# One-rounding quantisation in the mx layer, and causal attention stepped one sequence at a time

## The chip, the cores and the metric

One program on one core of a Trainium2 chip, in one launch. The metric is the device time of that core in microseconds. Its engines are named as in the profile: PE (TensorE; PEld is its weight load), DVE (VectorE), ACT (ScalarE), POOL (GpSimd) and SP (SyncE, which issues DMAs). Every engine runs its own instructions in order; they meet at semaphores.

## What is computed

Sixteen sequences of 256 tokens with 128 features pass through twelve stages (`load`, `gla`, `swiglu`, `mx_linear`, `causal_attention`, `router1`, `experts1`, `rope_attention`, `ternary_mlp`, `mamba`, `router3`, `experts3`). Every layer works on normalised rows and adds its result to `x`. Two stages matter here.

`mx_linear` quantises its input rows and its weight in blocks of 32 to the nearest value of a 6-bit grid (exact ties go down) and multiplies:

```python
def _mx_quantize(t, eps=1e-30):
    rows, K = t.shape
    blocks = t.reshape(rows, K // BLOCK_SIZE, BLOCK_SIZE)
    scales = jnp.maximum(jnp.max(jnp.abs(blocks), axis=-1) / FP6_E2M3_MAX, eps)
    q = _nearest_on_grid(blocks / scales[..., None], _GRID)
    return (q, scales)
```

`causal_attention` is, for each sequence, a single head of width 128: q, k and v are products of the normalised rows with `Wq`, `Wk`, `Wv` plus biases, the scores of a token with itself and earlier tokens go through a softmax, the weighted sum of v goes through `Wo`, plus a bias. Since the weights of a row sum to 1, the bias of v adds the same vector, bias times `Wo`, to every row of the result.

## The kernel before

`x` stays in SBUF, [128 partitions, 32 tiles of 128]; a sequence is two tiles. `g.mv` holds mean and variance of every row. Between two stages `Signals.close` (L56 to L62) lets POOL clear each semaphore of the stage, and all engines wait for that.

Both stages begin with `Norm`: DVE adds epsilon to the 32 variance columns, POOL raises them all to the power -0.5 (L205, `g.rs`), and DVE waits for it. `normalised` (L958) then makes the normalised rows of a sequence with two DVE instructions (L961). Both stages take two sequences, u = 0 and 1, per turn of a loop, eight turns in all, and work through each operation for u = 0, then for u = 1. Both end a turn with `Finish.vector` (L234 to L241), the statistics of the new rows of `x`, on DVE.

`mx_linear`: a turn on DVE is `quantised(i + 1)`, then `added(i)`. `quantised` is a `Chain` of 15 steps, each waiting for the step before of its own sequence: normalise, and in `mx_quantise` block maxima, scale, reciprocal, multiply; two clamps and two subtractions that cut a value in three parts; and for all three parts (768 elements per partition) a rounding (L998), its error (L1002), a test for ties (L1006) and a correction (L1010); then two additions and the scale. PE transposes the result (L1095), ACT copies it (L1083), PE multiplies with `wT` (L1103) and adds the bias by a product with a row of ones (L1104, a contraction over one row), and DVE adds it to `x` (L1063).

`causal_attention`: each sequence has four PSUM banks of its own, reused within a turn. Order of a turn: PE projects q, k (L1245, L1246) and v with its bias by a row of ones (L1252, L1253), ACT copies q and k out (L1213, L1214), PE makes scores (L1257, L1258), DVE masks them (L1159), takes maxima (L1163, L1164) and negates them (L1167), ACT takes exponentials (L1218, L1220), PE transposes (L1263), ACT copies (L1224), PE makes the context (L1270 to L1272), DVE copies it (L1175), PE multiplies with `Wo` (L1277), DVE divides and adds the bias (L1181), adds to `x` (L1187) and does the statistics. The normalised and transposed tokens of the next turn are made in the middle of this one. PE's v products of the next turn wait for this turn's result.

## Time and profile before

| what | value |
|---|---|
| median of 3 runs | 3184.25 us (3179.88 to 3189.71) |
| the profiled execution | 3185.84 us, span 3184.0 us |
| PE, DVE, ACT, POOL busy | 71%, 62%, 40%, 36% of the span |
| granted clock of PE, mean over the span | 0.841 |
| `mx_linear`, first to last instruction | 951.86 to 1098.24 us |
| `causal_attention`, first to last instruction | 1100.50 to 1235.27 us |

The stages follow one another with a stop of all engines between them, so the busy shares of the whole span say little of the two stages that the change touches; they are read from views of their own windows. A row `A:B` of a windows view gives a stretch's length, each engine's busy time in it with its number of instructions, the mean granted clock of PE (1.00 is 2.4 GHz, 0.50 is 1.2 GHz), the DMA engines' share and GB/s.

### The profile page before, as it was taken

What the parts mean: (1) busy time and instruction counts of PE and PEld (TensorE: products, weight loads), DVE (VectorE), ACT (ScalarE), POOL (GpSimd) and SP (SyncE); (2) the same over time, 40 slices, a digit from 0 to 9 for tenths busy, and PEclk for the clock granted to TensorE, in tenths of its full rate; (3) what the DMA queues carried; (4) which work ended last, traced back from release to release, by engine and by line L of the source; (5) the groups of instructions that cost most, each with busy time, mean ns of one, the idle gap of its engine ahead of it and who ended that gap; (6) DMA issues with size and microseconds to landing.
All of it is one profiled execution on the core that took longest, in us unless ns stands there. A gap on an engine that the chain in (4) does not pass through costs nothing. (4 is left out here: it accounts for less than half of the span.)

```text
span 3184.0 us, 47196 instructions
## 1 busy us (share of the span) xinstructions
PE 2253.1 (71%) x15094; PEld 1544.5 (49%) x15094; DVE 1972.1 (62%) x5353; ACT 1271.6 (40%) x2663; POOL 1153.3 (36%) x1205
## 2 busy tenths in 40 slices
PE   2899999999883485149189885748888889651290
PEld 0566666666672364037155553635555555440170
DVE  3677777777669754201466663858888888744016
ACT  2455454554330042013044553337777777410130
POOL 2342342433210001545211111137777777513551
PEclk9899999999995587579578887869999999855595
DMA  7300000000010000112323231000000000000122
GB/s 212 94 1 0 0 0 0 0 0 0 14 47 0 0 0 0 34 56 64 90 70 78 66 96 39 0 1 1 0 0 0 0 0 0 1 0 22 50 62 79
DMA packets 105855, 93.75 MB, mean 29 GB/s; under 512 B 12268, under 2 KB 92294, under 8 KB 105606
## 3 DMA queue, kind: packets, MB, share of 16 engines
q1 hardware_dynamic: 98086, 76.85, 8.8%
q0 software_dynamic: 7680, 15.81, 1.5%
q8 instruction: 45, 0.74, 0.1%
q14 instruction: 44, 0.36, 0.0%
HBM read 62.15 MB, written 46.26 MB: 34 GB/s over the span
## 5 line engine op out<-in xcount | busy, mean ns | idle before, releaser
L2713 POOL TENSOR_SCALAR mb_w<-mb_duT,mb_bT 128x256 f32<-128x256 f32 x512 | 463.8, 924 | 144.9 <-PE bank L2723 133.6
L2649 DVE TENSOR_TENSOR_SCAN mb_hs<-mb_dA,bank 128x512 f32<-128x512 f32 x256 | 300.6, 1203 | 31.5 <-issue 24.6
L38 POOL TENSOR_TENSOR scrap<-ones 128x1 f32<-128x1 f32 x96 | 19.8, 207 | 814.0 <-DVE gla_ss L420 487.4
L2742 PE MATMUL bank<-mb_hc,ident 128*128 128x512 f32 x512 | 251.6, 614 | 24.7 <-DVE mb_hc L2659 23.5
L1993 DVE TENSOR_REDUCE ra_mx<-bank 128x2 f32<-128x512 f32 x256 | 166.7, 687 | 99.5 <-PE bank L1870 98.1
L2704 ACT ACTIVATE mb_dA<-mb_delta,mb_A 128x255 f32<-128x255 f32 x512 | 217.6, 494 | 3.6 <-DVE mb_hs L2649 3.4
L2079 ACT ACTIVATE ra_pT<-bank 128x512 f32<-128x512 f32 x256 | 139.4, 596 | 129.4 <-PE bank L1890 128.5
L1644 ACT ACTIVATE e_hid<-bank,e_b 128x512 f32<-128x512 f32 (+1 forms) x128 | 81.1, 634 | 234.5 <-PE bank L1663 231.5
L2723 PE MATMUL bank<-ident,mb_w 128*128 128x128 f32 x1024 | 149.4, 280 | 35.6 <-DVE mb_hs L2649 26.2
L1627 POOL DMA_INDIRECT results<-e_y,e_x x112 | 107.2, 957 | 144.6 <-DVE e_y L1698 119.6
L1655 PE MATMUL bank<-ident,e_x 128*128 128x128 f32 x112 | 18.8, 292 | 197.3 <-DMA e_x<-queue 197.3
L2659 DVE TENSOR_TENSOR mb_hc<-mb_hs,bank 128x1024 f32<-128x1024 f32 x128 | 152.8, 1194 | 0.0
L2723 PEld LDWEIGHTS bank<-ident,mb_w 128*128 128x128 f32 x1024 | 117.0, 145 | 58.5 <-issue 45.3
L546 DVE COPY_PREDICATED gla_sT<-c_seen,bank 128x384 f32<-128x384 int32 x256 | 134.4, 576 | 12.1 <-issue 12.1
L2742 PEld LDWEIGHTS bank<-mb_hc,ident 128*128 128x128 f32 x512 | 88.1, 192 | 106.8 <-issue 62.2
L1692 DVE COPY e_xT<-bank 128x512 f32<-128x512 f32 (+1 forms) x32 | 19.7, 616 | 185.9 <-PE bank L1655 185.8
L532 DVE TENSOR_TENSOR gla_qm<-bank,gla_ex 128x256 f32<-128x256 f32 x128 | 53.9, 421 | 123.3 <-ACT gla_en L514 123.3
L1698 DVE TENSOR_TENSOR e_y<-bank,e_b 128x512 f32<-128x512 f32 (+1 forms) x32 | 20.0, 625 | 166.4 <-PE bank L1673 166.4
L1870 PE MATMUL bank<-ra_k,ra_q 48*128 48x256 bf16 x512 | 97.5, 304 | 33.4 <-DMA ra_q<-rope_rows 26.2
L1889 PE MATMUL bank<-ra_q,ra_k 48*128 48x256 bf16 x512 | 111.3, 298 | 9.5 <-ACT ra_neg L2072 8.3
L420 DVE TENSOR_REDUCE gla_ss<-gla_sq 128x8 f32<-128x512 f32 x128 | 87.0, 679 | 42.4 <-ACT gla_sq L398 40.5
L387 ACT ACTIVATE gla_az<-gla_az 128x512 f32<-128x512 f32 x64 | 40.3, 630 | 179.0 <-DVE gla_az L415 179.0
(516 smaller groups left out, 6234.8 us busy)
## 6 DMA issues: line engine op xcount, KB each, us to landing
results<-const_empty SPq DMA_DIRECT2D x2, 4096.0 KB
e_got<-results SPq DMA_DIRECT2D x32, 256.0 KB, 3.3
rope_rows<-ra_part SPq DMA_DIRECT2D x48, 128.0 KB, 2.0
ra_k<-rope_rows SPq DMA_DIRECT2D x32, 192.0 KB, 3.3
ra_q<-rope_rows SPq DMA_DIRECT2D x32, 192.0 KB, 4.3
queue<-const_spare_rows SPq DMA_DIRECT2D x1, 4128.0 KB
...
```

Of the source, the lines that this page charges most:

```text
L546: dve.copy_predicated(sT[b][:, hd, :], g.seen[:, :], SC[hd][:, 0:3 * P]).then_inc(sc_ready, 1)
L1627: pool.indirect_dma_start(out=results[:, :], in_=y[u % YR][:, t, :], in_offset=None, out_offset=bass.IndirectOffsetOnAxis(ap=x[e % XR][:, ...
L1870: ins = pe.matmul(MX[a][:, t * 256:(t + 1) * 256], qz[k][rows, p, t * P:(t + 1) * P], kk[k][rows, p, :], start=True, stop=True)
L1889: pe.matmul(out, kk[k][rows, p, t * P:(t + 1) * P], qz[k][rows, p, :], start=True, stop=False)
L1993: dve.tensor_reduce(mx[:, :, a, p], halves(MX[a]), AXX, ALU.max).then_inc(mx_ready, 1)
L2079: act.activation(pT[p % 4][a][:, :, :], halves(SB[a]), ACT.Exp, scale=SC).then_inc(p_ready, 1)
L2649: dve.tensor_tensor_scan(hs[n // 2 % 2][:, n % 2, :, :].rearrange("p c t -> p (c t)"), dA[n % RD][:, :, :].rearrange("p c t -> p (c t)"), ...
L2659: dve.tensor_tensor(hc[grp % 2][:, :, :, :], hs[grp % 2][:, :, :, :], RC[grp % 2][:, :].rearrange("p (n t) -> p n t", n=2).unsqueeze(2) .b ...
L2704: ins = act.activation(dA[n % RD][:, c, 1:SEQ], delta[k][:, c, 1:SEQ], ACT.Exp, scale=A[:, c, n:n + 1])
L2713: ins = pool.tensor_scalar(w[n % RH][:, h, :], duT[k][:, h, :], bT[k][:, h, n:n + 1], None, ALU.mult)
L2723: ins = pe.transpose(DB[n % 2][:, c * 256 + h * P:c * 256 + (h + 1) * P], w[n % RH][:, h, c * P:(c + 1) * P], g.ident[:, :])
L2742: ins = pe.matmul(YB[:, :], g.ident[:, :], hc[grp % 2][:, j, :, :].rearrange("p c t -> p (c t)"), start=(n == 0), stop=(n == NS - 1))
```

## The change

In `mx_quantise`, the three parts are gone. The power of two of each value (its exponent bits, by a bitwise and; at least 8) is kept in `p`, its inverse is made by a bitwise exclusive or, the value is multiplied with it, rounded once by adding a large constant in two ways of which the lower result is kept, multiplied back with `p` and scaled. This makes 13 steps, without normalising. Normalising moves to ACT as one activation per tile (`normalised_rows`), the addition of `x` moves to PE as a product with the identity, and ACT copies the sum back to `x`. The power -0.5 is taken in two parts, 4 tiles and then 28.

In `causal_attention` each purpose has one PSUM bank (`XT, QK, VB, SB, PT, CB, OB`), used by all sequences in turn; SBUF tiles stay doubled. A step works on one sequence s: PE projects s+1, makes the result of s-1, transposes the weights of s and the tokens of s+2, makes the scores of s+1 and the context of s. Semaphores are counted per sequence. Normalising and the copy of the context move from DVE to ACT. The bias of v is multiplied with `Wo` once, ahead of the steps, and added to the output bias (`bo`). The rolled loops make 5 turns of two steps; 2 steps ahead of them and 4 behind them are written out.

```diff
--- before.py
+++ after.py
...
-def mx_quantise(chain, x, y, amax, sc, z, r, t, n):
...
+def mx_quantise(chain, x, out, amax, sc, back, y, p, w, v, n):
...
-    return lambda: (chain.step(lambda u: dve.tensor_tensor(y[u][:, 0:w], y[u][:, 0:w], r[u][:, 2, 0:w], ALU.add)),
-                    chain.step(lambda u: dve.tensor_tensor(blocks(x[u]), blocks(y[u][:, 0:w]), wide(sc[u][:, :]),
-                                                           ALU.mult)))
+    chain.step(lambda u: dve.tensor_scalar(back[u][:, 0:n], sc[u][:, 0:n], 0.5, None, ALU.mult))
+    chain.step(lambda u: dve.reciprocal(amax[u][:, 0:n], sc[u][:, 0:n]))
+    chain.step(lambda u: dve.tensor_tensor(blocks(cols(y[u])), blocks(x[u]), wide(amax[u][:, 0:n]), ALU.mult))
+
+    chain.step(lambda u: dve.tensor_scalar(cols(p[u]).bitcast(I32), cols(y[u]).bitcast(I32), MX_EXP, None,
+                                           ALU.bitwise_and))
+    chain.step(lambda u: dve.tensor_scalar(cols(p[u]), cols(p[u]), 8.0, None, ALU.max))
+    chain.step(lambda u: dve.tensor_scalar(cols(w[u]).bitcast(I32), cols(p[u]).bitcast(I32), MX_EXP, None,
+                                           ALU.bitwise_xor))
+    chain.step(lambda u: dve.tensor_tensor(cols(w[u]), cols(y[u]), cols(w[u]), ALU.mult))
+
+    chain.step(lambda u: dve.tensor_scalar(cols(v[u]), cols(w[u]), MX_ODD, -0.25, ALU.add, ALU.add))
+    chain.step(lambda u: dve.scalar_tensor_tensor(out=cols(v[u]), in0=cols(w[u]), scalar=MX_EVEN, in1=cols(v[u]),
+                                                  op0=ALU.add, op1=ALU.min))
+    chain.step(lambda u: dve.scalar_tensor_tensor(out=cols(v[u]), in0=cols(v[u]), scalar=-MX_EVEN, in1=cols(p[u]),
+                                                  op0=ALU.add, op1=ALU.mult))
+    chain.step(lambda u: dve.tensor_tensor(blocks(out[u]), blocks(cols(v[u])), wide(back[u][:, 0:n]), ALU.mult))
...
 def mx_linear(nc, g):
...
         def _(dve):
...
-            mx_quantise(ch, w, [y[0]], [amax[0][:, 0:4]], [sc[0][:, 0:4]], z, r, t, 4)()
+            moments = g.mv[:, :].rearrange("p (t k) -> p t k", k=2)
+            dve.tensor_scalar(var[:, :], moments[:, :, 1], LN_EPS, None, ALU.add).then_inc(var_ready, 1)
+            dve.wait_ge(rs_ready, 1)
+            dve.scalar_tensor_tensor(out=nmr[:, early], in0=moments[:, early, 0], scalar=-1.0, in1=g.rs[:, early],
+                                     op0=ALU.mult, op1=ALU.mult).then_inc(nmr_ready, 1)
+            ch = Chain(dve, [wq_steps], 0, MX_STEPS, items=(0,))
+            mx_quantise(ch, [g.mx_w[:, :]], [wd[:, :]], amax, sc, back, y, p, w, v, 4)
             ch.close()
...
+            dve.wait_ge(rs_ready, 2)
+            dve.scalar_tensor_tensor(out=nmr[:, later], in0=moments[:, later, 0], scalar=-1.0, in1=g.rs[:, later],
+                                     op0=ALU.mult, op1=ALU.mult).then_inc(nmr_ready, 1)
...
             def quantised(i):
-                if not isinstance(i, int):
-                    for u in U:
+                for u in U:
+                    if not isinstance(i, int):
                         dve.wait_ge(xT_psum[u], i)
-                ch = Chain(dve, steps, i, MX_STEPS + 3)
-                ch.step(lambda u: normalised(dve, g, xn[u], i * 2 + u, g.rs))
-                mx_quantise(ch, flat, y, amax, sc, z, r, t, 8)()
+                    dve.wait_ge(xn_ready[u], i + 1)
+                ch = Chain(dve, steps, i, MX_STEPS)
+                mx_quantise(ch, x_in, x_out, amax, sc, back, y, p, w, v, 8)
                 ch.close()
+
+            def finished(i):
+                for u in U:
+                    fin.vector(dve, u, i, i * 2 + u, x_ready[u])
+
+            quantised(0)
+            with dve.Fori(0, NSEQ // 2 - 1) as i:
+                quantised(i + 1)
+                finished(i)
+            finished(NSEQ // 2 - 1)
+
+        @block.gpsimd
+        def _(pool):
+            pool.wait_ge(var_ready, 1)
+            for part in (early, later):
+                pool.tensor_tensor(g.rs[:, part], var[:, part], g.neg_half[:, part], ALU.pow).then_inc(rs_ready, 1)
+
...
+            def normalised_rows(i):
+                for u in U:
+                    s = i * 2 + u
+                    if not isinstance(i, int) or i:
+                        act.wait_ge(steps[u], (i - 1) * MX_STEPS + MX_READ)
+                    for h in range(2):
+                        ins = act.activation(xn[u][:, h, :], g.x[:, ds(s * (2 * P) + h * P, P)], ACT.Identity,
+                                             bias=scale_of(nmr, s * 2 + h), scale=scale_of(g.rs, s * 2 + h))
+                    ins.then_inc(xn_ready[u], 1)
+
+            def transposed(i):
+                for u in U:
+                    act.wait_ge(xT_psum[u], i + 1)
+                    act.activation(xT[u][:, :], T[u][:, 0:256], ACT.Copy).then_inc(xT_ready[u], 1)
...
+                    act.wait_ge(o_psum[u], i + 1)
+                    act.activation(g.x[:, seq_cols(s)], O[u][:, 0:256], ACT.Copy).then_inc(x_ready[u], 1)
+
+            act.wait_ge(nmr_ready, 1)
+            normalised_rows(0)
+            act.wait_ge(wT_psum, 1)
+            act.activation(wT[:, :], T[0][:, 0:P], ACT.Copy).then_inc(wT_ready, 1)
+            act.wait_ge(nmr_ready, 2)
+            normalised_rows(1)
+            transposed(0)
+            added(0)
+            with act.Fori(1, NSEQ // 2 - 1) as i:
+                normalised_rows(i + 1)
+                transposed(i)
                 added(i)
+            transposed(NSEQ // 2 - 1)
             added(NSEQ // 2 - 1)
...
             def product(i):
                 for u in U:
-                    pe.wait_ge(steps[u], i * (MX_STEPS + 3) + MX_STEPS + 3)
+                    pe.wait_ge(steps[u], i * MX_STEPS + MX_STEPS)
                     for h in range(2):
-                        ins = pe.transpose(T[u][:, h * P:(h + 1) * P], xn[u][:, h, :], g.ident[:, :])
+                        ins = pe.transpose(T[u][:, h * P:(h + 1) * P], xd[u][:, h, :], g.ident[:, :])
                     ins.then_inc(xT_psum[u], 1)
                 for u in U:
+                    s = i * 2 + u
                     if not isinstance(i, int) or i:
                         pe.wait_ge(x_ready[u], i)
                     pe.wait_ge(xT_ready[u], i + 1)
                     for h in range(2):
                         o = O[u][:, h * P:(h + 1) * P]
                         pe.matmul(o, xT[u][:, h * P:(h + 1) * P], wT[:, :], start=True, stop=False)
+                        pe.matmul(o, g.ident[:, :], g.x[:, ds(s * (2 * P) + h * P, P)], start=False, stop=False)
                         ins = pe.matmul(o, g.ones[0:1, :], g.mx_b[:, :], start=False, stop=True)
                     ins.then_inc(o_psum[u], 1)
...
+
+    def over(s, n):
+        return not isinstance(s, int) or s >= n
+
+    def pe_tokens(pe, s, u):
+        pe.wait_ge(xn_ready, s + 1)
+        if over(s, 1):
+            pe.wait_ge(xT_ready, s)
+        for h in range(2):
+            ins = pe.transpose(XT[:, h * P:(h + 1) * P], xn[u][:, h, :], g.ident[:, :])
+        ins.then_inc(xT_psum, 1)
+
+    def pe_project(pe, s, u):
+        pe.wait_ge(xT_ready, s + 1)
+        if over(s, 1):
+            pe.wait_ge(qk_ready, s)
+        pe.matmul(QK[:, 0:256], g.l1_Wq[:, :], xT[u][:, :], start=True, stop=True)
+        pe.matmul(QK[:, 256:512], g.l1_Wk[:, :], xT[u][:, :], start=True, stop=True).then_inc(qk_psum, 1)
+        if over(s, 1):
+            pe.wait_ge(v_ready, s)
+        for h in range(2):
+            ins = pe.matmul(VB[:, h * P:(h + 1) * P], xT[u][:, h * P:(h + 1) * P], g.l1_Wv[:, :], start=True,
+                            stop=True)
+        ins.then_inc(v_psum, 1)
+
+    def pe_scores(pe, s, u):
+        pe.wait_ge(qk_ready, s + 1)
+        if over(s, 1):
+            pe.wait_ge(sm_ready, s)
+        pe.matmul(SB[:, 0:P], q[u][:, 0:P], k[u][:, 0:P], start=True, stop=True)
+        pe.matmul(SB[:, P:3 * P], q[u][:, P:2 * P], k[u][:, :], start=True, stop=True).then_inc(s_psum, 1)
+
...
+            pe.wait_ge(cT_ready, s)
+        pe.matmul(CB[:, 0:P], v[u][:, 0:P], pT[u][:, 0:P], start=True, stop=True)
+        pe.matmul(CB[:, P:2 * P], v[u][:, 0:P], pT[u][:, P:2 * P], start=True, stop=False)
+        pe.matmul(CB[:, P:2 * P], v[u][:, P:2 * P], pT[u][:, 2 * P:3 * P], start=False, stop=True).then_inc(c_psum, 1)
+
+    def pe_result(pe, s, u):
+        pe.wait_ge(cT_ready, s + 1)
+        if over(s, 1):
+            pe.wait_ge(z_ready, s)
+        for h in range(2):
+            ins = pe.matmul(OB[:, h * P:(h + 1) * P], cT[u][:, h * P:(h + 1) * P], g.l1_Wo[:, :], start=True, stop=True)
+        ins.then_inc(o_psum, 1)
+
...
+    def act_exp(act, s, u):
+        act.wait_ge(nmx_ready, s + 1)
+        if over(s, 2):
+            act.wait_ge(rinv_ready, s - 1)
+        act.activation(sm[u][:, 0:P], sm[u][:, 0:P], ACT.Exp, bias=mx[u][:, 0:1], accum_out=sums[u][:, 0:1])
+        act.activation(sm[u][:, P:3 * P], sm[u][:, P:3 * P], ACT.Exp, bias=mx[u][:, 1:2],
+                       accum_out=sums[u][:, 1:2]).then_inc(p_ready, 1)
...
+    def dve_maxima(dve, s, u):
+        dve.wait_ge(sm_ready, s + 1)
+        if over(s, 2):
+            dve.wait_ge(p_ready, s - 1)
+        dve.tensor_reduce(mx[u][:, 0:1], sm[u][:, 0:P], AXX, ALU.max)
+        dve.tensor_reduce(mx[u][:, 1:2], sm[u][:, P:3 * P], AXX, ALU.max).then_inc(mx_ready, 1)
+
+    def dve_offsets(dve, s, u):
+        dve.wait_ge(mx_ready, s + 1)
+        dve.tensor_scalar(mx[u][:, :], mx[u][:, :], -1.0, None, ALU.mult).then_inc(nmx_ready, 1)
...
+    def dve_divided(dve, s, u):
+        dve.wait_ge(rinv_ready, s + 1)
+        dve.wait_ge(o_psum, s + 1)
+        for h in range(2):
+            ins = dve.scalar_tensor_tensor(out=z[u][:, h * P:(h + 1) * P], in0=OB[:, h * P:(h + 1) * P],
+                                           scalar=rinv[u][:, h:h + 1], in1=bo[:, :], op0=ALU.mult, op1=ALU.add)
+        ins.then_inc(z_ready, 1)
+
...
+    def pe_step(pe, s, u, back=True, on=True, far=True):
+        w = 1 - u
+        if on:
+            pe_project(pe, s + 1, w)
+        if back:
+            pe_result(pe, s - 1, w)
+        pe_weights(pe, s, u)
+        if far:
+            pe_tokens(pe, s + 2, u)
+        if on:
+            pe_scores(pe, s + 1, w)
+        pe_context(pe, s, u)
+
+    def act_step(act, s, u, back=True, on=True, far=True, farther=True):
+        w = 1 - u
+        if back:
+            act_context(act, s - 1, w)
+        act_exp(act, s, u)
+        if on:
+            act_qk(act, s + 1, w)
+        act_weights(act, s, u)
+        if far:
+            act_tokens(act, s + 2, u)
+        if farther:
+            act_normalised(act, s + 3, w)
+
+    def dve_step(dve, s, u, back=True, on=True):
+        w = 1 - u
+        if on:
+            dve_values(dve, s + 1, w)
+        dve_inverse(dve, s, u)
+        if back:
+            dve_divided(dve, s - 1, w)
+            dve_result(dve, s - 1, w)
+            dve_stats(dve, s - 1, w)
+        if on:
+            dve_masked(dve, s + 1, w)
+        if back:
+            dve_moments(dve, s - 1, w)
+        if on:
+            dve_maxima(dve, s + 1, w)
+        if back:
+            dve_keep(dve, s - 1, w)
+        if on:
+            dve_offsets(dve, s + 1, w)
+
+    def steps(eng, step, ends):
+        step(eng, 0, 0, back=False)
+        step(eng, 1, 1)
+        with eng.Fori(1, NSEQ // 2 - 2) as i:
+            for u in U:
+                step(eng, i * 2 + u, u)
+        for s in range(NSEQ - 4, NSEQ):
+            step(eng, s, s % 2, **{name: s + n <= last for name, n in ends.items()})
 
     with nc.Block() as block:
...
+                dve.scalar_tensor_tensor(out=nmr[:, tiles], in0=moments[:, tiles, 0], scalar=-1.0, in1=g.rs[:, tiles],
+                                         op0=ALU.mult, op1=ALU.mult).then_inc(nmr_ready, 1)
+                if part == 0:
+                    dve.wait_ge(bv_psum, 1)
+                    dve.tensor_copy(bv[:, :], OB[:, 0:1]).then_inc(bv_ready, 1)
+                    dve_values(dve, 0, 0)
+                    dve_masked(dve, 0, 0)
+                    dve_maxima(dve, 0, 0)
+                    dve_offsets(dve, 0, 0)
+                    dve.wait_ge(bo_psum, 1)
+                    dve.tensor_tensor(bo[:, :], OB[:, P:2 * P], g.l1_bo[:, :], ALU.add).then_inc(bo_ready, 1)
+            dve.wait_ge(bo_ready, 1)
+            steps(dve, dve_step, {"on": 1})
+            dve_divided(dve, last, 1)
+            dve_result(dve, last, 1)
+            dve_stats(dve, last, 1)
+            dve_moments(dve, last, 1)
+            dve_keep(dve, last, 1)
 
         @block.gpsimd
...
-                attended(i)
-            attended(NSEQ // 2 - 1, False)
+            pe.matmul(OB[:, 0:1], g.l1_bv[:, :], g.ones[0:1, 0:1], start=True, stop=True).then_inc(bv_psum, 1)
+            pe_tokens(pe, 0, 0)
+            pe_project(pe, 0, 0)
+            pe_tokens(pe, 1, 1)
+            pe_scores(pe, 0, 0)
+            pe.wait_ge(bv_ready, 1)
+            pe.matmul(OB[:, P:2 * P], bv[:, 0:1].broadcast_to([P, P]), g.l1_Wo[:, :], start=True, stop=True)\
+                .then_inc(bo_psum, 1)
+            pe.wait_ge(bo_ready, 1)
+            steps(pe, pe_step, {"on": 1, "far": 2})
+            pe_result(pe, last, 1)
     sb.close()
     sig.close()
```

## Rows read from the trace of the kernel before

**Rows 1.** Windows: start of mx_linear, the rest of it, causal_attention.

```profile
951.86:963.65 11.79, 0.47 (x1) 0.18 (x1) 5.24 (x21) 0.00 (x0) 5.43 (x1) 0.50 0.00 0
963.65:1098.24 134.59, 55.76 (x160) 37.40 (x160) 122.56 (x465) 6.13 (x16) 0.00 (x0) 0.50 0.00 0
1100.50:1235.27 134.77, 100.70 (x496) 79.77 (x496) 72.99 (x306) 49.51 (x135) 5.42 (x1) 0.83 0.00 0
```

**Rows 2.** Timeline of mx_linear on DVE: start, length, instruction, [idle before].

```profile
990.82 0.74 DVE L1063 TENSOR_TENSOR x<-bank,x 128x256 f32 x2
...
1007.22 0.74 DVE L1063 TENSOR_TENSOR x<-bank,x 128x256 f32 x2
...
1010.69 1.18 DVE L961 TENSOR_SCALAR mx_xn<-x,mv,rs 128x128 f32 x4 [0.72 <-issue]
...
1011.78 0.74 DVE L982 TENSOR_REDUCE mx_amax<-mx_xn 128x8 f32<-128x256 f32 x2
...
1012.88 0.76 DVE L986 TENSOR_TENSOR mx_y<-mx_xn,mx_amax 128x256 f32<-128x256 f32 x2
1013.56 0.28 DVE L989 TENSOR_SCALAR mx_z<-mx_y 128x256 f32<-128x256 f32 x1
...
1015.71 1.29 DVE L998 TENSOR_SCALAR mx_r<-mx_z 128x256 f32<-128x256 f32 x6
```

**Rows 3.** Groups by line and form: the nearest other shapes for new instructions.

```profile
L2510 DVE SCALAR_TENSOR_TENSOR mb_delta<-mb_z,mb_az 128x512 f32<-128x512 f32 x16 | 11.1, 692 | 22.1 <-ACT mb_az L2588 22.1
...
L1635 POOL TENSOR_TENSOR e_rs<-e_ve,neg_half 128x4 f32<-128x4 f32 x8 | 8.1, 1011 | 58.1 <-DVE e_ve L1740 58.1
```

**Rows 4.** Timeline of PE at half clock, last products of mx_linear.

```profile
1090.14 0.79 PE L1103 MATMUL bank<-mx_wT,mx_xT 128*128 128x128 f32 x2
...
1090.86 0.79 PE L1104 MATMUL bank<-mx_b,ones 1*128 1x128 f32 x2
```

**Rows 5.** Timeline of PE at half clock, last turn of causal_attention.

```profile
1229.34 0.55 PEld L1270 LDWEIGHTS bank<-ca_pT,ca_v 128*128 128x128 f32 x2
...
1229.76 0.55 PEld L1271 LDWEIGHTS bank<-ca_pT,ca_v 128*128 128x128 f32 x2
```

**Rows 6.** Timeline of ACT in an earlier stage: a table load and its activation.

```profile
117.22 1.28 ACT L513 ACT_TABLE_LOAD   x1
118.52 0.39 ACT L513 ACTIVATE gla_ex<-bank 128x264 f32<-128x264 f32 x1
```

**Rows 7.** Waits at the starts of causal_attention and of the router.

```profile
DVE ca_norm_t L189 <- PEq L57: 2.3, 1, 2.3
...
DVE r_norm_t L189 <- PEq L57: 4.4, 1, 4.4
```

**Rows 8.** Timeline of causal_attention at full clock: one turn's length, and its legs.

```profile
1172.85 0.42 DVE L1175 COPY ca_cT<-bank 128x256 f32<-128x256 f32 x1 [1.55 <-PE bank L1272]
...
1175.62 0.47 ACT L1213 ACTIVATE ca_q<-bank,ca_bqs 128x256 f32<-128x256 f32 x1 [1.54 <-PE bank L1246]
...
1179.69 0.49 PE L1257 MATMUL bank<-ca_k,ca_q 128*128 128x128 f32 x2
...
1180.65 1.21 DVE L1159 TENSOR_TENSOR ca_sm<-bank,c_causal 128x384 f32<-128x384 f32 x2 [0.43 <-PE bank L1258]
...
1183.01 0.40 ACT L1218 ACTIVATE ca_sm<-ca_sm,ca_mx 128x128 f32<-128x128 f32 x1 [3.84 <-DVE ca_mx L1167]
...
1184.05 0.31 PEld L1263 LDWEIGHTS bank<-ident,ca_sm 128*128 128x128 f32 x3 [3.19 <-ACT ca_sm L1220]
...
1186.62 0.42 DVE L1175 COPY ca_cT<-bank 128x256 f32<-128x256 f32 x1 [1.55 <-PE bank L1272]
```

**Rows 9.** Windows within causal_attention: PE's granted clock against its busy time.

```profile
1136.00:1140.00 4.00, 1.22 (x6) 0.57 (x5) 3.37 (x14) 1.87 (x9) 0.00 (x0) 0.80 0.00 0
...
1180.00:1195.00 15.00, 11.89 (x70) 9.16 (x68) 9.87 (x40) 6.24 (x17) 0.00 (x0) 1.00 0.00 0
1112.00:1120.00 8.00, 8.00 (x23) 5.88 (x22) 1.41 (x3) 0.84 (x2) 0.00 (x0) 0.50 0.00 0
```

327 lines of the change are left out of this document (131 added, 196 removed).

## The prediction

> **What bounds the kernel now.** The page says only that PE is busy 71% of the span. Both changed stages stand alone between two stops of all engines, so I read their windows first [rows 1]. In `mx_linear` DVE is busy 122.56 of 134.59 us and PE has 0.50 of its clock throughout: DVE bounds it, and only shorter DVE work helps. `causal_attention` takes 134.77 us with PE busy 100.70 and DVE 72.99: no engine is full. The timeline shows why: two sequences pass through the same legs one behind the other, one turn taking 1186.62 - 1172.85 = 13.77 us at full clock, 6.9 per sequence, with DVE idle 1.55 us ahead of the context copy while PE works, PE idle 3.19 us ahead of the weights' transposes while DVE and ACT work, and ACT idle 3.84 us ahead of the exponential [rows 8]. It is a chain of latencies, with PE as the longest user.
>
> **mx_linear: the chain.** A turn takes 1007.22 - 990.82 = 16.40 us. From 1007.22 to 1010.69 come two additions, the statistics and a loop gap of 0.72, 3.47 us together; the other 12.93 are the 15 steps [rows 2]. Prices for both sequences of a step, start to start: a two-source instruction of 256 elements 1013.56 - 1012.88 = 0.68; a one-source one 0.40 (six in 1.29, the last 0.28, so 0.20 each); block maxima, scale and reciprocal 1012.88 - 1011.78 = 1.10, of which a tiny step is (1.10 - 0.68) / 2 = 0.21 [rows 2]. The new chain has maxima and three tiny steps, 1.31; five two-source steps, 3.40; four one-source steps, 1.62 with rounding: 6.33 us. Two prices are not shown. No wide integer instruction with one source is in the trace; below it is the f32 one-source 0.40, above it the two-source 0.68. I take 0.40, the nearest in operands and size; the upper end adds 2 x 0.28 x 8 = 4.5 us. The scalar-tensor-tensor takes 0.692 us for 512 elements [rows 3], which agrees with 0.42 for 256; I price it as two-source. The page "Vector Engine (DVE) Microarchitecture Reference" of the Trainium skill, section 5.1, lets any one-source instruction between SBUF tiles take the two-port mode; by that rule the integer steps cost 0.40.
>
> So eight chains save 8 x 6.60 = 52.8 us, and the additions, 0.67 a turn, leave DVE in six turns: 4.0. Normalising in ACT is at no cost to DVE, since ACT was busy 6.13 us in the whole stage [rows 1]; it is queued behind `added`, which I come to below.
>
> **mx_linear: both ends.** Before, the first chain starts 11.79 us into the stage: a power of 5.43 us, then the weight's chain [rows 1]. A power over 4 columns takes 1.01 us [rows 3]; the weight's 13 steps (about 3.7 us alone, one-item steps) now lie beside the power of the other 28 columns, which ends near 5.8, and the first chain starts near 6.3: 5.5 saved. At the end PE and ACT are exposed. PE at half clock passes from a 128-row product to a one-row product in 1090.86 - 1090.14 = 0.72 us [rows 4], and between two 128-row products in 0.42 [rows 5]. A tile now has `xT`, identity, ones: 0.42 + 0.72 + 0.72 = 1.86, four tiles 7.5, transposes and copy 1.2, the last copy 0.4, the statistics 0.95: 10.1 us after the last chain, where it was 9.1. Loss 1.0.
>
> Sum for `mx_linear`: 52.8 + 4.0 + 5.5 - 1.0 = 61.3 us. The turn becomes 6.33 + 2.80 = 9.13 us, and PE needs 8.7 of it, ACT some 4 plus a table load. ACT ends `added` 9.1 after a chain, loads a table if the loop head asks for one (1.28), normalises in 1.5, and is done 11.9 after that chain; DVE wants the rows at 9.13 + 2.80 = 11.9. It just fits, so it is late next.
>
> **causal_attention: the step.** A step is a cycle: exponential of s, copy of q and k of s+1, scores of s+1, mask, maxima, negation, then exponential of s+1. Legs [rows 8]: ACT is through with an exponential after 0.89 (its data reach PE after 1184.05 - 1183.01 = 1.04); q and k 0.37 + 0.47 = 0.84 and 0.06 to PE; scores 1180.65 - 1179.69 = 0.96. From mask to exponential two sequences take 1183.01 - 1180.65 = 2.36; for one, with the old sequence's aggregates between, it lies between 1.18 and 2.36, and instruction by instruction (mask 0.6, aggregates 0.25, maxima 0.6, negation 0.2) I take 1.65. Sum 4.40 us against 6.9. Beside it must fit: on DVE the v copy, inverse, division, addition and two statistics, which are through some 2.8 us after the exponential's start, just when the scores come; on ACT weights, tokens, normalising (0.74) and the context copy, through just ahead of the next exponential; on PE 3.7 us at full clock (q, k 0.86, v 0.44, scores 0.65, transposes 0.6, context 0.66, result 0.5). The v products lose their one-row partner, which by the same switch made a v of 0.42 per product out of 0.22: 1.2 us of PE per sequence gone.
>
> A loop head asks for one table load in each of 5 turns of two steps; ACT then comes to the exponential 0.6 late, 3.0 us in all, with a load of 1.28 and its activation 118.52 - 117.22 = 1.30 after its start [rows 6]. The page "ScalarE: Activation LUTs" of the Trainium skill, "What ACT_TABLE_LOAD costs", adds a drain of 1.38 us to each load; the row shows 0.02. By the page five turns here would cost 6.9 us more.
>
> At half clock PE needs 7.2 a step and bounds it. Before, the clock was 0.50 over 1112 to 1120 with PE busy all 8 us, and fell again in a stretch with 1.22 of 4 us busy; over 1180 to 1195, 11.89 of 15 busy, it stayed 1.00 [rows 9]. The new step has no such idle stretch and no one-row products, so I expect a later clock mostly at 1.00, with one to three steps at half clock at first.
>
> **causal_attention: the sum.** Ahead of the steps 10.0 us (power of 4 columns 1.3, normalise, transpose, project, scores, mask, two bias products at half clock); the first step 7.2; fourteen of 4.40, 61.6; table loads 3.0; from the last exponential to the last statistic 7.0: 88.8, and 97.2 with three more steps at half clock. I take 95, a saving of 39.8. Fewer semaphores, 30 for 50: DVE waited 2.3 us at the stop that clears 24 and 4.4 at the one that clears 50 [rows 7], 0.08 each, so 1.7 less.
>
> Total 61.3 + 39.8 + 1.7 = 102.8. The profiled execution took 3185.84, its span 3184.0; 3185.84 - 102.8 = 3083.0, and as it lies 1.6 over the median, I forecast 3082 us.
>
> **Rivals.**
> - *PE or ACT bounds the mx turn* (0.08). If identity products also cost 0.72, four tiles cost 1.2 us more, the turn grows to some 10.3: 3082 + 8 x 1.15 = 3091. For it: 8.7 of 9.13 is thin. Against: rows 5 show 0.42 for just such neighbours.
> - *Half clock throughout causal_attention* (0.10). 16 x 7.2 + 17 = 132: 3119. For it: 8 busy us at 0.50; against: the rise later in that stage [rows 9].
> - *Cross waits in the step* (0.07). DVE reaches the mask late, as inverse and division stand in its queue ahead of it and wait for ACT and PE; a step of 6.0 adds 24: 3106.
> - *Each table load stops ACT longer* (0.03). A stop the size of a load, 5 loads here and 6 halved in `mx_linear`, is 8 x 1.3 = 10: 3092. The row speaks against it. The drain of the skill's page would be this rival.
> - *Slower* (0.02). One bank per purpose makes each step wait for all legs of its sequence, so nothing overlaps. The old turn is such a pass, 13.77 for two; at 13 per step the stage takes 16 x 13 + 3 = 211, 76 more than before: 3185.8 - 61.3 - 1.7 + 76 = 3199. It decides from (134.8 + 63 - 17) / 16 = 11.3 us a step. Against it: the code has PE project s+1 before it needs the weights of s.
> - *No change* (0.01) would need a step near 11.
> The likeliest case has the rest, 0.69, with its own range 3066 to 3100.
>
> **Range and chances.** Below, `mx_linear` with PE at full clock (-3), attention at 89 with no table cost (-9) and smaller gaps give 3066, with a margin for the estimated fill 3062. Above, slow integers (+4.5), three half-clock steps (+2) and cross waits (+24) reach 3113, and 3116 leaves out little but the clock rival. Three in a thousand (0.3%, about what a measurement of this kernel can tell from no change) is 9.6 us, far inside the forecast: faster 0.97, same 0.01, slower 0.02.
>
> **What would show it.** In the new profile: an mx chain of 6.3 us and a turn of 9.1 us; the integer steps at 0.28 us an instruction; `mx_linear` some 85 us long; exponentials 4.4 to 5.0 us apart, the stage some 95 us long at a clock near 0.9; the router's wait about 2.7 us. Wrong would be: DVE waiting for normalised rows in `mx_linear`, integer steps at 0.41, exponentials 6 us or more apart, or 0.50 of clock far into the attention.

## The result, and the profile after

The changed kernel takes 3082.48 us, the median of four runs (3071.34 to 3087.23), against 3185.32 before: a ratio of 0.9673 [0.9642, 0.9704]. The forecast was 3082. Two of its terms were off, though, by 7 and by 13 us in opposite directions, and most of what follows is about them.

The profiled execution is the one of 3071.34 us, the fastest of the four, with a span of 3069.2. Windows of the changed kernel: `mx_linear`, `causal_attention`, all that follows, and three stretches of the attention. They answer to [rows 1] and [rows 9].

```profile
951.17:1043.39 92.22, 69.38 (x225) 51.48 (x225) 68.81 (x336) 24.35 (x65) 5.77 (x2) 0.50 0.00 0
1045.51:1127.16 81.65, 69.50 (x436) 59.02 (x436) 55.78 (x262) 58.43 (x177) 5.77 (x2) 0.94 0.00 1
...
1130.14:3069.20 1939.06, 1275.64 (x7685) 861.66 (x7685) 1110.24 (x2513) 794.40 (x1646) 840.06 (x981) 0.80 0.12 33
...
1045.50:1049.50 4.00, 1.61 (x5) 1.13 (x6) 0.50 (x4) 1.68 (x5) 3.73 (x2) 0.50 0.01 4
1049.50:1053.50 4.00, 3.85 (x16) 3.05 (x15) 0.76 (x2) 1.57 (x4) 2.04 (x1) 0.70 0.00 0
1053.50:1121.50 68.00, 61.64 (x406) 53.15 (x406) 50.89 (x238) 54.31 (x167) 0.00 (x0) 1.00 0.00 0
```

`mx_linear` went from 146.38 to 92.22 us and is no longer full on DVE, which is busy 68.81 us of it; PE, at 0.50, is now as busy as DVE. `causal_attention` went from 134.77 to 81.65 us, and PE's clock is 1.00 from 8 us into the stage up to 1121.5, a step before its end. The wait that answers to [rows 7] shrank by 1.4:

```profile
DVE r_norm_t L189 <- PEq L57: 3.0, 1, 3.0
```

The timeline of `mx_linear` after, one turn on three engines; it answers to [rows 2].

```profile
957.36 0.75 DVE L989 TENSOR_REDUCE mx_amax<-mx_xn 128x8 f32<-128x256 f32 x2
...
1005.11 0.74 DVE L989 TENSOR_REDUCE mx_amax<-mx_xn 128x8 f32<-128x256 f32 x2 [0.69 <-ACT mx_xn L1084]
1005.30 0.80 PE L1133 MATMUL bank<-mx_wT,mx_xT 128*128 128x128 f32 x2 [1.62 <-ACT mx_xT L1091]
...
1007.11 0.49 DVE L996 TENSOR_SCALAR mx_p<-mx_y 128x256 int32<-128x256 int32 x2
...
1011.42 0.28 DVE L234 BATCH_NORM_STATS2 mx_fin_st<-x 128x6 f32 x1
...
1012.79 1.11 PE L1124 MATMUL bank<-ident,mx_xd 128*128 128x128 f32 x4
1013.01 0.38 ACT L1097 ACTIVATE x<-bank 128x256 f32 x1 [3.36 <-PE bank L1135]
1013.56 1.65 ACT L1084 ACTIVATE mx_xn<-x,mx_nmr,rs 128x128 f32 x4 [0.17 <-issue]
1015.11 0.63 ACT L1091 ACTIVATE mx_xT<-bank 128x256 f32<-128x256 f32 x2
1015.33 0.74 DVE L989 TENSOR_REDUCE mx_amax<-mx_xn 128x8 f32<-128x256 f32 x2 [0.69 <-ACT mx_xn L1084]
1015.52 0.79 PE L1133 MATMUL bank<-mx_wT,mx_xT 128*128 128x128 f32 x2 [1.61 <-ACT mx_xT L1091]
```

The chain is 1011.42 - 1005.11 = 6.31 us, but the turn is 1015.33 - 1005.11 = 10.22. What ends each wait closes a loop through two engines, ACT and PE. ACT has stood 3.36 us before `added`, which waits for PE's products; behind it in its queue are the normalising of the next rows and the copy of `xT`. After `added` ACT first normalises four tiles (1013.56 to 1015.11), for which DVE then waits 0.69, and only then copies `xT`, for which PE has been idle 1.61 us. From the last copy of `added` in one turn to the same in the next it takes 0.38 + 0.17, then 1.55 of normalising, 0.41 to the first product, and 7.7 of products at half clock: 10.2.

The timeline of `causal_attention` after; it answers to [rows 8].

```profile
1055.79 1.28 ACT L1247 ACT_TABLE_LOAD   x1
1057.08 0.40 ACT L1247 ACTIVATE ca_sm<-ca_sm,ca_mx 128x128 f32<-128x128 f32 x1
...
1078.13 0.40 ACT L1247 ACTIVATE ca_sm<-ca_sm,ca_mx 128x128 f32<-128x128 f32 x1 [0.41 <-DVE ca_mx L1284]
...
1079.02 0.45 ACT L1240 ACTIVATE ca_q<-bank,ca_bqs 128x256 f32<-128x256 f32 x1
...
1079.89 0.49 PE L1194 MATMUL bank<-ca_k,ca_q 128*128 128x128 f32 x2
...
1080.85 0.56 DVE L1273 TENSOR_TENSOR ca_sm<-bank,c_causal 128x384 f32<-128x384 f32 x1
...
1082.39 0.40 ACT L1247 ACTIVATE ca_sm<-ca_sm,ca_mx 128x128 f32<-128x128 f32 x1 [0.41 <-DVE ca_mx L1284]
...
1120.17 0.40 ACT L1247 ACTIVATE ca_sm<-ca_sm,ca_mx 128x128 f32<-128x128 f32 x1 [0.41 <-DVE ca_mx L1284]
```

One step is 1082.39 - 1078.13 = 4.26 us, and the fifteen from the first exponential to the last are (1120.17 - 1057.08) / 15 = 4.21 each: exponential to q copy 0.89, q and k to scores 0.87, scores to mask 0.96, mask to exponential 1.54. The table load at 1055.79 is the only one of the stage; its activation starts 0.01 us after its end.

### The profile page after: what moved, and what is told of

Its sections match the earlier page's. It is cut to its first block and busy times, and to the rows that moved or that the text cites. A ratio compares the mean times of both kernels' runs of the same rounds, so it can differ in the third digit from the quotient of the medians.

```text
span 3069.2 us, 47277 instructions
## 1 busy us (share of the span) xinstructions
PE 2227.3 (73%) x15098; PEld 1531.8 (50%) x15098; DVE 1896.1 (62%) x5160; ACT 1299.1 (42%) x2754; POOL 1156.5 (38%) x1207
## 5 line engine op out<-in xcount | busy, mean ns | idle before, releaser
L2140 DVE TENSOR_REDUCE ra_mx<-bank 128x2 f32<-128x512 f32 x256 | 166.3, 686 | 95.9 <-PE bank L2017 94.3
L546 DVE COPY_PREDICATED gla_sT<-c_seen,bank 128x384 f32<-128x384 int32 x256 | 134.3, 576 | 12.1 <-issue 12.1
L2889 PEld LDWEIGHTS bank<-mb_hc,ident 128*128 128x128 f32 x512 | 88.2, 192 | 106.7 <-issue 62.4
L1802 PEld LDWEIGHTS bank<-ident,e_x 128*128 128x128 f32 x112 | 14.4, 152 | 201.7 <-DMA e_x<-queue 200.8
```

The costliest lines, as they stand in the source:

```text
L546: dve.copy_predicated(sT[b][:, hd, :], g.seen[:, :], SC[hd][:, 0:3 * P]).then_inc(sc_ready, 1)
L2140: dve.tensor_reduce(mx[:, :, a, p], halves(MX[a]), AXX, ALU.max).then_inc(mx_ready, 1)
L2889: ins = pe.matmul(YB[:, :], g.ident[:, :], hc[grp % 2][:, j, :, :].rearrange("p c t -> p (c t)"), start=(n == 0), stop=(n == NS - 1))
```

## The experiments

Stage lengths in this table are from the start of `mx_linear` to that of `causal_attention`, from there to the router's, and from there to the end of the span, each in the one profiled execution. The runs e1 to e4, e5 to e8 and e9 to e12 each shared a chip and their runs of the kernel before (3188.61, 3184.31 and 3188.19 us). A stage length is of one execution, a median of several, so the two need not differ by the same amount.

| kernel | median us | ratio [95%] | mx | attention | rest |
|---|---|---|---|---|---|
| before | 3185.3 | | 148.6 | 139.2 | 1944.3 |
| after | 3082.5 | 0.9673 [0.9642, 0.9704] | 94.3 | 84.6 | 1939.1 |
| e1 | 3125.3 | 0.9809 [0.9781, 0.9837] | 94.3 | 133.5 | 1943.9 |
| e2 | 3140.4 | 0.9855 [0.9825, 0.9885] | 148.7 | 86.7 | 1953.7 |
| e3 | 3133.7 | 0.9837 [0.9813, 0.9861] | 102.6 | 128.3 | 1947.3 |
| e4 | 3176.6 | 0.9968 [0.9956, 0.9980] | 148.6 | 127.1 | 1947.4 |
| e5 | 3082.3 | 0.9677 [0.9662, 0.9693] | 94.3 | 86.8 | 1948.5 |
| e6 | 3077.0 | 0.9662 [0.9648, 0.9675] | 89.3 | 84.9 | 1952.0 |
| e7 | 3074.1 | 0.9651 [0.9636, 0.9665] | 83.0 | 86.1 | 1951.7 |
| e8 | 3073.8 | 0.9652 [0.9637, 0.9666] | 85.0 | 84.1 | 1947.2 |
| e9 | 3100.4 | 0.9734 [0.9714, 0.9754] | 94.3 | 103.1 | 1947.5 |
| e10 | 3094.8 | 0.9702 [0.9682, 0.9723] | 94.3 | 100.1 | 1950.3 |
| e11 | 3186.5 (one execution) | | 148.7 | 136.2 | 1945.8 |
| e12 | 3092.6 | 0.9702 [0.9685, 0.9719] | 97.4 | 91.0 | 1952.7 |

### Which half of the change gives what

**e1** is the changed kernel with the attention of before, **e2** the kernel before with the attention of after.

```diff
 e1: after.py
-def causal_attention(nc, g):   # seven banks, one sequence a step
+def causal_attention(nc, g):   # of before.py
 e2: before.py
-def causal_attention(nc, g):
+def causal_attention(nc, g):   # of after.py
```

> Only mx_linear and its quantiser are the new ones, causal_attention is the old one. The change's own trace has mx_linear at 92.2 us (951.17 to 1043.39) where it was 146.4. If the stages are separate, this run is 54 us faster than before, about 3131 us, and its attention stays near 134.8 us. Rival: the busier PE of the new mx_linear hands the attention a warmer clock; then the old attention is over 5 us shorter here too, and part of what I put down to the attention's new order belongs to mx_linear.

> Only causal_attention is the new one, mx_linear is the old one. Separate stages: 53 us from the attention and 1.5 us from fewer semaphores to clear, about 3131 us, with the attention near 82 us and exponentials 4.2 us apart from the first on. Rival (clock handed over by the new mx_linear): the attention begins at half clock for some steps of 7 us and takes 90 us or more.

e1 was 63.3 us under the kernel before, where 54 were expected, and e2 48.2, where 54.5 were. `mx_linear` has its 94.3 us in e1 as in after, and the new attention its 86.7 in e2 as in e5, so each half carries its own gain. (In e2 one step took 5.74 us; the half clock for steps of 7 us and the 90 us of e2's rival did not come.) The two gains add up to 111.5 us, 9 more than the whole change brings. Of these, the profiles show 5.7: the old attention took 133.5 us in e1 and 139.2 before, with the same instructions. No stage shows the remaining 3. Its windows in e1, the whole stage and its first 20 us:

```profile
1046.50:1180.00 133.50, 95.09 (x496) 74.57 (x496) 73.06 (x306) 49.40 (x135) 5.43 (x1) 0.87 0.00 0
1046.50:1066.50 20.00, 13.33 (x36) 9.29 (x36) 2.88 (x10) 3.73 (x7) 5.43 (x1) 0.50 0.00 1
```

and in **e3**, which has only the new quantiser in the old frame of `mx_linear`:

```diff
 before.py, mx_linear
-                ch = Chain(dve, steps, i, MX_STEPS + 3)
+                ch = Chain(dve, steps, i, MX_STEPS + 1)
                 ch.step(lambda u: normalised(dve, g, xn[u], i * 2 + u, g.rs))
-                mx_quantise(ch, flat, y, amax, sc, z, r, t, 8)()
+                mx_quantise(ch, flat, flat, amax, sc, back, y, p, w, v, 8)
```

> The old kernel with the new quantiser alone; normalising, the addition to x and the old order stay on DVE. My prices: chain 6.33 + 1.09 for normalising = 7.4 us, turn 7.4 + 3.5 = 10.9 us, the stage 44 to 46 us shorter than 146.4, so about 3140 us. The change's own turn is 10.22 us, so all that moves to ACT and PE would be worth only some 0.7 us a turn. Rival: additions wait for PE (7.1 us of products against a chain of 7.4) and the turn is 12 us or more; then the moves are worth much more.

```profile
1055.10:1183.40 128.30, 89.28 (x496) 70.77 (x496) 73.02 (x306) 48.98 (x135) 5.42 (x1) 0.91 0.00 0
1055.10:1075.10 20.00, 10.45 (x48) 7.68 (x49) 5.97 (x22) 6.37 (x18) 5.42 (x1) 0.75 0.00 1
```

The old stage is the shorter the more of it PE has its full clock: a mean of 0.82, 0.87 and 0.91 goes with 139.2, 133.5 and 128.3 us. So the gain of the new attention is 42 to 55 us, by how the old one was caught. The 5.7 us in e1 are what its rival asked for (over 5 us, from the busier PE of the new `mx_linear`), but that cause doesn't fit: in e3 PE was busy only 56 of the 100 us of `mx_linear`, against 69 of 91 in e1, and the old attention was shorter still. What makes the clock rise earlier in one execution than in another isn't shown; `mx_linear` ran at 0.50 ahead of all three. This is also why e3 is 55 us faster and not the 45 expected: its stage of `mx_linear` gained what was forecast. e3 also divides the gain of `mx_linear`: the shorter chain alone brings 46.0 of its 54.3 us, with a turn of 10.85 us, and the move of normalising, addition and power 8.3 more.

**e4** takes only the bias of v out of the old attention's steps.

```diff
 before.py, causal_attention
-                        pe.matmul(o, xT[u][:, h * P:(h + 1) * P], g.l1_Wv[:, :], start=True, stop=False)
-                        ins = pe.matmul(o, g.ones[0:1, :], g.l1_bv[:, :], start=False, stop=True)
+                        ins = pe.matmul(o, xT[u][:, h * P:(h + 1) * P], g.l1_Wv[:, :], start=True, stop=True)
```

> The old attention with only the bias of v taken through the output (no one-row products in the turns); the order of two sequences per turn stays. If PE's v products are on the turn's chain, a turn at full clock goes from 13.77 to 11.3 us and the stage is 20 to 25 us shorter, less about 2 for the two products ahead: about 3165 us. Rival: the stagger alone is what counts, the v products lie beside ACT's copies, and the stage is less than 5 us shorter.

The stage is 12.1 us shorter in the profiled execution, and so are the medians by 12.0, while the ratio of 0.9968 gives 10.2: about half of what was expected. It did not come from the turn that the expectation meant: where the old turn took 13.77 us at full clock, e4's takes 13.74. What e4 lacks are the longer turns, 15.1 to 16.1 us each, that the kernel before has while its clock is low, and its first mask comes 4.5 us earlier in the stage. The windows within one of e4's turns, and PE's first product after the idle stretch, in e4 and then before:

```profile
1169.50:1171.50 2.00, 0.04 (x1) 0.00 (x0) 2.00 (x6) 0.00 (x0) 0.00 (x0) 1.00 0.00 0
1171.50:1173.50 2.00, 0.14 (x1) 0.14 (x2) 1.87 (x9) 1.18 (x5) 0.00 (x0) 1.00 0.00 0
1173.50:1175.50 2.00, 1.67 (x9) 1.44 (x9) 0.48 (x3) 1.38 (x6) 0.00 (x0) 0.57 0.00 0
1175.50:1177.30 1.80, 1.80 (x11) 1.80 (x10) 0.00 (x0) 1.74 (x4) 0.00 (x0) 0.53 0.00 0
```

```profile
1173.36 0.55 PE L1268 MATMUL bank<-ident,ca_sm 128*128 128x128 f32 x3 [3.83 <-ACT ca_sm L1226]
...
1184.05 0.55 PE L1263 MATMUL bank<-ident,ca_sm 128*128 128x128 f32 x3 [2.78 <-ACT ca_sm L1220]
```

With the bias products gone PE waits 3.83 us for the weights, where it waited 2.78 (the 3.19 of [rows 8] is the wait of the weight load), and the transposes and context products behind that wait run at 0.57 and 0.53. From the first transpose to the copy of the context e4 takes 1177.31 - 1173.36 = 3.95 us, the kernel before 1186.62 - 1184.05 = 2.57. From that copy to the next mask it is the other way round, 6.60 for 7.80, and mask to transpose takes 3.20 for 3.40. What PE gained by having less to do it lost by doing the next legs at half clock. The new order has the same products without that wait, and there the fold shortens a step at full clock by 0.63 us (e10). Over the whole stage the two are near each other all the same, 13.3 us there and 12.1 here.

**e5** is the changed kernel once more, as the neighbour of e6 to e8.

> The changed kernel once more, for the spread: its four times lie between 3071 and 3087 us and its profiled execution (3071.3) is the lowest. If the two changed stages vary (clock phases), mx_linear or the attention differ by 3 us or more from 92.2 and 81.7 in this profile. Rival: the spread lies in other stages (those with transfers), and both stages are within 1 us of these.

3082.3 us, the same. The two profiled executions are 11.8 us apart: none of it lies in `mx_linear` (94.3 both times), 2.2 in the attention (86.8 against 84.6), where the clock fell once more after its first rise, and 9.4 in the stages behind it, which the change doesn't touch. So it was neither of the two that were expected: the spread lies mostly in the rest, but the attention has some.

### What sets the turn of mx_linear

**e6** lets ACT copy `xT` first.

```diff
             with act.Fori(1, NSEQ // 2 - 1) as i:
-                normalised_rows(i + 1)
                 transposed(i)
+                normalised_rows(i + 1)
                 added(i)
```

> The changed kernel with ACT copying the transposed rows of a turn before it normalises the next ones. Theory: in the change PE waits 2.0 us a turn for that copy, behind 1.65 us of normalising in ACT's queue, and PE bounds the turn (10.22 us). With the copy first PE needs 7.5 + 1.5, the turn falls to about 9.1 us, bounded by DVE, the stage loses 7 to 8 us: about 3075 us. Rival: PE's products themselves bound the turn, which stays above 9.8 us, under 3 us gained; or DVE now waits for the later normalised rows and nothing is gained.

The turn fell from 10.22 to 9.34 us, the stage by 5.0, the medians by 5.3 (0.9662 against 0.9677, whose intervals overlap, though each of e6's five times lies below each of e5's four). That is less than the 7 to 8 us and the turn of 9.1 that were expected, since DVE still waits, 0.86 before each chain, now for rows that are normalised behind the copies. **e7** leaves the order and makes the bias product one of 128 rows, of which 127 are zero (`brow`, filled once ahead of the loop).

```diff
-                        ins = pe.matmul(o, g.ones[0:1, :], g.mx_b[:, :], start=False, stop=True)
+                        ins = pe.matmul(o, g.ones[:, :], brow[:, :], start=False, stop=True)
```

> The changed kernel with the bias of mx_linear added by a 128-row product (a tile that holds the bias in its first row and zeros below, and ones) in place of the one-row product. Theory: at half clock a passage between a 128-row and a one-row product costs 0.72 us against 0.42, so a tile falls from 1.86 to 1.28, four tiles by 2.3 us; the turn is then bounded by DVE at about 9.1 us: about 3074 us, and the last products end 2.3 us earlier. Rival: the price belongs to three products per tile, not to the one-row form; then a 128-row bias costs the same and the turn stays at 10.2 us.

**e8** has both edits.

> Both edits, copy first on ACT and the 128-row bias. DVE bounds the turn: 6.33 + 2.80 = 9.1 us, no better than either alone by more than 1 us a turn, the tail another 2.3 us shorter: about 3072 us. If the turn falls clearly under 9.0, DVE was not the bound that I named; if the granted clock of mx_linear rises above 0.5, the one-row products were what held it down.

Windows of 67 us in the middle of `mx_linear`: in after,

```profile
963.00:1030.00 67.00, 56.99 (x186) 42.55 (x187) 54.10 (x264) 18.77 (x51) 0.00 (x0) 0.50 0.00 0
```

in e6,

```profile
963.00:1030.00 67.00, 61.41 (x200) 45.34 (x200) 57.24 (x277) 20.22 (x53) 0.00 (x0) 0.50 0.00 0
```

and in e7, where chains start 9.02 us apart, with nothing but the loop's own gap before them.

```profile
963.00:1030.00 67.00, 41.72 (x218) 37.06 (x219) 58.47 (x289) 21.52 (x55) 0.00 (x0) 0.75 0.00 0
```

e7 gains 11.3 us in the stage and 8.2 in the medians. PE does more turns' work in 41.72 busy us than in 56.99, for two reasons: the clock is 0.75, not 0.50, and no product stands next to a one-row one. The timelines part them. Two tiles' first products, both at a clock of 0.50, in after and then in e7:

```profile
1007.17 0.80 PE L1133 MATMUL bank<-mx_wT,mx_xT 128*128 128x128 f32 x2
...
1009.05 0.80 PE L1133 MATMUL bank<-mx_wT,mx_xT 128*128 128x128 f32 x2
...
1000.62 0.63 PE L1139 MATMUL bank<-mx_wT,mx_xT 128*128 128x128 f32 x2
...
1001.90 0.63 PE L1139 MATMUL bank<-mx_wT,mx_xT 128*128 128x128 f32 x2
```

A tile takes 1.88 us in after and 1.28 in e7 at the same half clock, as its expectation had it, so four tiles give back 2.4 us without any help from the clock. With 1.1 of transposes that leaves PE an estimated 6.2 of 9.0 us: the wider product alone takes PE off the bound, and the clock comes on top. In e6 PE was busy 61.41 of 67 us and kept 0.50 all the same. With PE out of the way DVE's 9.02 is what bounds the turn, so the order adds nothing. In e8 it costs a little: DVE waits 0.77 to 0.86 us for its rows in four of its turns, which take 9.25 to 9.35, and the stage is 85.0 us against e7's 83.0; the medians are the same. Each of the five times of e7, and of e8, lies below each of e5's four, by ratios of 0.9651 [0.9636, 0.9665] for e7 and 0.9677 [0.9662, 0.9693] for e5, whose intervals just touch. e7 and e8 are the fastest versions found.

### What sets the step of the attention

**e9** makes ACT copy the transposed weights ahead of q and k. If the step is the cycle through exponential, q copy and scores, whatever delays the q copy comes back in full.

```diff
         act_exp(act, s, u)
+        act_weights(act, s, u)
         if on:
             act_qk(act, s + 1, w)
-        act_weights(act, s, u)
```

> The changed kernel with ACT copying the weights of s ahead of q and k of s+1. Theory: the step of 4.2 us is the cycle exponential, q and k, scores, mask, maxima, exponential, and nothing else bounds it; ACT now stands 0.2 us for the transposes and copies 0.4 us ahead of q and k, so the step grows to 4.8 to 4.9 us, 16 steps some 10 us, about 3092 us. Rival: DVE (18.8 of 25 us busy) or PE (21.9 of 25) sets the step by its amount of work; then moving ACT's copy leaves it within 0.1 us of 4.2.

```profile
1085.43 0.40 ACT L1247 ACTIVATE ca_sm<-ca_sm,ca_mx 128x128 f32<-128x128 f32 x1 [0.41 <-DVE ca_mx L1284]
...
1087.44 0.47 ACT L1240 ACTIVATE ca_q<-bank,ca_bqs 128x256 f32<-128x256 f32 x1
...
1089.29 0.56 DVE L1273 TENSOR_TENSOR ca_sm<-bank,c_causal 128x384 f32<-128x384 f32 x1 [1.06 <-PE bank L1195]
...
1090.83 0.40 ACT L1247 ACTIVATE ca_sm<-ca_sm,ca_mx 128x128 f32<-128x128 f32 x1 [0.41 <-DVE ca_mx L1284]
```

The q copy starts 2.01 us after the exponential, where it was 0.89: 1.12 later. The steps are (1138.87 - 1058.70) / 15 = 5.34 us on the mean, 1.14 longer, while PE and DVE have the same work as before: neither sets the step by its amount of work. The cycle is as forecast; the delay was about twice the 0.6 us that was expected, as ACT waits 0.64 for PE's transposes and then copies the weights for 0.39. The stage grew by 16 to 19 us, against e5 and after, and the medians by 18.

**e10** puts the bias of v back into the steps, as one-row products, and leaves its product with `Wo` out of `bo`.

```diff
-            ins = pe.matmul(VB[:, h * P:(h + 1) * P], xT[u][:, h * P:(h + 1) * P], g.l1_Wv[:, :], start=True,
-                            stop=True)
+            pe.matmul(VB[:, h * P:(h + 1) * P], xT[u][:, h * P:(h + 1) * P], g.l1_Wv[:, :], start=True, stop=False)
+            ins = pe.matmul(VB[:, h * P:(h + 1) * P], g.ones[0:1, :], g.l1_bv[:, :], start=False, stop=True)
```

> The changed kernel with the bias of v added by one-row products in every step again, in the staggered order (the output bias is not corrected for it). By my prices PE's work per step grows from 3.7 to 4.9 us at full clock, PE becomes the bound, the step is 4.9 to 5.2 us and the stage some 14 us longer, about 3096 us; if the one-row products also hold the clock down for longer, as in mx_linear, the stage is 20 us longer or more. Rival: PE has slack enough and the step stays under 4.5 us; then the bias edit is worth nothing to the new order.

Windows of e10, its first 20 us of the stage and 20 late ones, and the same late ones of after:

```profile
1046.10:1066.10 20.00, 16.42 (x51) 12.77 (x52) 3.89 (x16) 8.68 (x21) 5.77 (x2) 0.50 0.00 1
...
1090.00:1110.00 20.00, 20.00 (x130) 17.12 (x129) 13.82 (x67) 15.06 (x47) 0.00 (x0) 1.00 0.00 0
```

```profile
1090.00:1110.00 20.00, 19.27 (x129) 16.63 (x128) 15.84 (x76) 16.87 (x54) 0.00 (x0) 1.00 0.00 1
```

The step is 4.84 us and PE is never idle in the later window: here PE bounds it, and ACT waits 0.9 us for the maxima where it waited 0.41. In after PE is busy 19.27 of 20, 4.06 us of a step of 4.21. The cycle still sets the step, but PE lies 0.15 behind it, which the forecast's 3.7 us of PE work did not see. e10's stage is 13.3 us longer than e5's, more than 15 x 0.63 = 9.5, because its clock stays at 0.50 for the first 20 us, where after's rises within 8 and the other runs of the new attention have theirs up within 8 to 12: its first two steps take 6.54 and 6.68 us, e5's 4.81 and 5.11. The 20 us that the expectation set for that case were not reached.

**e11** (one execution, no interval) writes ACT's first turn of the old attention out ahead of the loop.

```diff
-            with act.Fori(0, NSEQ // 2 - 1) as i:
+            attended(0)
+            with act.Fori(1, NSEQ // 2 - 1) as i:
                 attended(i)
```

> The old kernel with the first turn of the attention written out on ACT ahead of its loop. Theory: the table load of each turn came from entering the loop with no table of the right set loaded; with one turn ahead of the loop there is 1 load in place of 7, as in the changed kernel, and the turn stays at 13.8 us at full clock, since ACT waited for PE there anyway. Rival: every loop head asks for a load; there are 7 again.

Groups of ACT in the attention, before and in e11:

```profile
L1213 ACT ACT_TABLE_LOAD x7 | 9.0, 1283 | 0.1
```

```profile
L1218 ACT ACT_TABLE_LOAD x1 | 1.3, 1283 | 0.0
```

Seven loads become one. In this kernel the loop loaded its table in every turn where it was entered without the exponential's table, and in none where a first exponential was written out ahead. The time doesn't show it, 3186.5 us, as far as one execution can tell: the six loads lay in ACT's idle time. The changed attention has its first steps written out, so it has one load, and the forecast's five were never there.

**e12** gives the power as 31 columns and then 1, in place of 4 and then 28, in both stages.

```diff
-    early = slice(0, 4)
-    later = slice(4, NTILE)
+    early = slice(0, NTILE - 1)
+    later = slice(NTILE - 1, NTILE)
```

> The changed kernel with the power -0.5 taken for 31 columns first and 1 after, in both stages, in place of 4 and 28. By my sum the first chain of mx_linear starts when 5.3 us of power and the weight's 3.7 us of steps are through one behind the other, some 3.5 us later, and the attention starts 4.2 us later: some 8 us more, about 3090 us. Rival: the fill behind it absorbs part, and it is under 4 us.

Timeline of e12, its first chain, in a stage that starts at 951.77:

```profile
961.05 0.74 DVE L989 TENSOR_REDUCE mx_amax<-mx_xn 128x8 f32<-128x256 f32 x2
```

The chain starts 9.3 us into the stage and not 6.2; `mx_linear` grew by 3.1 us and the attention by 4.2 over e5's. That is 7.3 us in the two stages, near the 8 expected, for the power in two parts. The medians of e12 and e5, measured on two chips, are 10 us apart, by their ratios 8.

## Why the prediction held, point by point

**The sum.** Forecast 102.8 us; between the medians lie 102.8, between e5 and its neighbour before 102.0. That exactness is luck, since two terms are off by more than their sum shows:

| term | forecast | measured |
|---|---|---|
| `mx_linear`, first to last instruction | 61.3 | 146.38 - 92.22 = 54.2 |
| `causal_attention`, first to last instruction | 39.8 | 134.77 - 81.65 = 53.1 |
| router's wait | 1.7 | 4.4 - 3.0 = 1.4 |
| all | 102.8 | 108.7 |

e5's two stages give 106.7 by the table's measure, its medians 102.0. The rest of the program, which is the same code in all kernels, is from 1939.1 to 1953.7 us long over the profiles, and 1944.3 in the one of before. So some 4 us of the stages' gain don't arrive in e5's time. On the mean the rest takes 1949.2 us in the nine profiles with the new attention and 1945.7 in the five with the old; with single profiles that vary by 15, whether it is really slower behind the new stages stays open. The forecast's last step has a slip of its own: 3083.0 less 1.6 is 3081.4.

**The chain of mx_linear: right.** 6.31 us for 6.33. The integer steps took 0.49 for two, 0.285 an instruction, the same as one-source f32. The rule of the Trainium skill's page "Vector Engine (DVE) Microarchitecture Reference", section 5.1, agrees; it gives the two-port mode to copies, casts and tensor-scalar instructions, which these are, and not to every one-source instruction, as the prediction words it. The first chain starts 957.36 - 951.17 = 6.2 us into the stage, for 6.3.

**The turn of mx_linear: the step that failed.** The prediction took the turn as 6.33 + 2.80 = 9.13, since PE needs 8.7 and ACT's rows arrive just when DVE wants them. PE's need was right: 7.5 of products and 1.11 of transposes, a tile taking 1.87 us for 1.86, though its three passages are 0.59, 0.56 and 0.72 and not 0.42, 0.72 and 0.72. What it left out is that PE's 8.7 are in two parts with ACT's copy between them, and that in ACT's queue `added` and the normalising stand in front of that copy. PE then takes its 8.6 plus 1.6 of waiting, 10.2. DVE waiting for normalised rows, which the prediction named as a sign of being wrong, is there with 0.69 us, and the stage is 92.2 us and not some 85. This is near the rival's 10.3, but by another cause: the rival had dearer identity products, and the tile as a whole was no dearer than forecast. e6 shortens the waiting by an exchange of two lines and e7 the length of the products, and at 9.02 us e7 shows DVE's bound where it was forecast. Up to the end of the last chain this cost 5.7 us, and the tail 1.4 (11.5 for 10.1): 7.1 in all.

**The attention: mechanism right, its allowances mis-sized.** The steps are 4.21 us for 4.40, with q copy, scores and mask on the path as forecast (e9). The last exponential to the last statistic took 7.0, as forecast. Of the 13.3 us that the stage is shorter than 95, 3.0 are the five table loads that don't exist (e11), 2.7 the shorter steps, 1.5 the way to the second exponential (11.6 us and then 4.2, for 10.0 and 7.2; the one table load, 1.28, is in the 11.6), and 6.2 the allowance for steps at half clock, of which there were none in this profile: the clock was 1.00 before the first exponential. In e5's it fell again, and two steps were 1.5 us longer together. The prediction's 3.19 us of idle PE before was the weight load's wait; the products waited 2.78. In e10 the first 20 us are at half clock, so such an allowance was no mistake in kind.

**The other rivals.** Half clock throughout: not in any run, a mean of 0.94 here. Cross waits: DVE came to the mask in time in after; from the second on, an exponential waits 0.39 to 0.41 us for DVE's negation alone. Longer stops at a table load: activation 0.01 us after the load, and the drain that the page "ScalarE: Activation LUTs" of the Trainium skill, "What ACT_TABLE_LOAD costs", gives isn't there. Slower: the step is 4.2, far from 11.3.

**The two ranges.** 3082.48 lies in both. The parts that the forecast sized wrongly cancel in part; with the turn at 10.2 and the attention at 82, the same reasoning would have given some 3076 by the profile before.
